# Windowed self-attention of a decoder in plain fp32 on heads padded to 32 rows, two units a step

## The reference

```python
qkv = hidden_states @ w_qkv.T
q, k, v = jnp.split(qkv, 3, axis=-1)
q = _rms_norm(q, q_norm_w); k = _rms_norm(k, k_norm_w)     # over all 256 columns
# 16 heads of 16 columns
q = _rope(q); k = _rope(k)
mask = (q_idx >= k_idx) & (q_idx - k_idx <= 127)
scores = jnp.where(mask, einsum('bhqd,bhkd->bhqk', q, k) / 4, -inf)
probs = softmax(scores)
out = einsum('bhqk,bhkd->bhqd', probs, v) @ w_o.T
```

## Time and profile before

| what | us |
|---|---|
| median of 3 runs | 1463.75 |
| the three runs | 1457.23, 1463.75, 1466.10 |
| the profiled execution, its own time | 1464.83 |
| its span, first to last instruction | 1463.0 |
| mean granted TensorE clock, share of full | 0.922 |
| instructions | 22043 |

### The profile page before, as it was taken

How to read it: one execution, slowest core, us unless ns; L and a number is a source line. 1 busy time by engine, 2 the same in 40 slices (tenths; PEclk the granted TensorE clock), 3 DMA queues, 4 the chain that set the end, 5 groups by cost and what they waited for, 6 DMA issues and landing times.

```text
span 1463.0 us, 22043 instructions
## 1 busy us (share of the span) xinstructions
PE 1228.0 (84%) x7024; PEld 833.0 (57%) x7024; DVE 924.3 (63%) x2269; ACT 590.8 (40%) x1524; POOL 547.2 (37%) x629
## 2 busy tenths in 40 slices
PE   7688998999869877689989999999999806988881
PEld 3554664677634365557768336643566705777770
DVE  1678886653697975839964877668765442544443
ACT  2247775884531102548820137621665122222220
POOL 2243773642242314525520004410343172444444
PEclk9899999999769978989997999999999957999996
DMA  7165994000001001010020000000400442544444
GB/s 284 56 225 169 327 316 135 2 1 1 30 1 43 1 1 72 0 58 2 2 107 17 0 0 1 2 0 1 201 2 35 181 175 69 84 85 81 82 75 104
DMA packets 69615, 110.75 MB, mean 76 GB/s; under 512 B 5056, under 2 KB 59840, under 8 KB 66240
## 3 DMA queue, kind: packets, MB, share of 16 engines
q1 hardware_dynamic: 58896, 96.62, 19.5%
q0 software_dynamic: 10608, 12.72, 5.7%
HBM read 57.41 MB, written 51.91 MB: 75 GB/s over the span
## 4 chain that ended last, share of the span: by engine, by line
PE 62%; DVE 18%; issue 6%; POOL 6%; DMA 4%; ACT 3%; SPq 0%; POOLq 0%; DVEq 0%; ACTq 0%
PE ps L692 8%; PE ps L681 6%; PE ps L967 6%; PE ps L701 4%; PE ps L673 4%; PE ps L674 3%; PE ps L1021 3%; PE ps L1018 3%; DMA sums<-mem 2%; PE ps L948 2%; PE ps L641 2%; PE ps L803 2%; POOL mem L1858 2%; DVE mem L1155 1%; PE ps L786 1%
## 5 line engine op out<-in xcount | busy, mean ns | idle before, releaser
L1858 POOL TENSOR_SCALAR mem<-mem 128x512 f32<-128x512 f32 x256 | 177.6, 698 | 388.6 <-DVE mem L1160 385.3
L1155 DVE TENSOR_REDUCE mem<-ps 128x1 f32<-128x512 f32 x256 | 175.2, 686 | 108.9 <-PE ps L674 100.4
L1670 ACT ACTIVATE mem<-ps,mem 128x512 f32<-128x512 f32 x256 | 177.1, 696 | 12.7 <-DVE mem L1155 12.1
L681 PE MATMUL ps<-mem 128*128 128x128 f32 x1024 | 159.0, 278 | 14.3 <-POOL mem L1858 13.4
L681 PEld LDWEIGHTS ps<-mem 128*128 128x128 f32 x1024 | 118.1, 141 | 69.5 <-POOL mem L1858 50.7
L1663 ACT ACTIVATE mem<-ps 128x512 f32<-128x512 f32 x192 | 116.0, 606 | 93.2 <-PE ps L681 92.7
L1924 POOL DMA_INDIRECT sums<-mem x63 | 97.1, 1541 | 128.3 <-DVE mem L1532 102.3
L673 PE MATMUL ps<-rounded_at 128*128 128x512 f32 x256 | 124.3, 486 | 11.8 <-DVE rounded_at L1144 10.4
L692 PE MATMUL ps<-mem 128*64 128x256 f32 x1024 | 125.8, 388 | 2.4 <-ACT mem L1663 2.4
L1868 POOL TENSOR_TENSOR mem<-mem 128x512 f32<-128x512 f32 x40 | 55.4, 1384 | 140.5 <-DVE mem L1196 140.4
L1638 ACT ACTIVATE rounded_at<-ps 64x512 fp32r<-64x512 f32 x64 | 37.8, 591 | 167.1 <-PE ps L950 154.3
(11 more groups left out here) (259 smaller groups left out, 2646.7 us busy)
## 6 DMA issues: line engine op xcount, KB each, us to landing
slots<-mem SPq DMA_DIRECT2D x15, 2312.0 KB, 9.9
mem<-in_f_w_dram SPq DMA_DIRECT2D x16, 1024.0 KB, 10.3
mem<-slots SPq DMA_DIRECT2D x63, 136.0 KB, 2.5
mem<-in_f_w_dram SPq DMA_DIRECT2D x24, 256.0 KB, 3.3
mem<-in_x_wq_dram SPq DMA_DIRECT2D x2, 2048.0 KB, 13.2
mem<-in_x_wo_dram SPq DMA_DIRECT2D x2, 2048.0 KB, 8.3
mem<-sums SPq DMA_DIRECT2D x8, 256.0 KB, 4.6
mem<-in_x_wqr_dram SPq DMA_DIRECT2D x1, 1536.0 KB, 6.7
```

Of the source, the lines that this page charges most:

```text
L681: mm = pe.transpose(ps[3 + j % 2][:, k * P:(k + 1) * P], PR[j % 6][:, k * P:(k + 1) * P], ident)
L1155: dve.tensor_reduce(nmax[:, i % 8:i % 8 + 1], ps[SB[lay][i % len(SB[lay])]][:, :], AX.X, ALU.max, negate=True)\
L1670: act.activation(PR[i % 6], ps[SB[lay][i % len(SB[lay])]][:, :], ACT.Exp, bias=nmax[:, i % 8:i % 8 + 1], accum_out=esum[:, i % 8:i % 8 + 1 ...
L1858: pool.tensor_scalar(PR[i % 6], PR[i % 6], rinv[:, i % 8:i % 8 + 1], 1.0, ALU.mult, ALU.mult)\
```

## The change

Only the fourth sublayer changes. There are no high and low parts any more: Q, K, V and the probabilities stay plain fp32, and their products have two passes. A head's 16 columns are padded with zeros to 32 (`QK1`), so four heads stand under each other after one transpose of 128 columns, at rows 0, 32, 64 and 96; a tile takes 8 transposes instead of 16, and one copy each by ACT and DVE instead of three and one. The banks of the transposed tiles are doubled. The cosine product moves from POOL to DVE; POOL clears the padding once and the padding of V at the end.

The loop goes over 24 pairs. The two units of a pair (hh = 0, 1) take heads at neighbouring row groups and write neighbouring banks of one double bank `pp`. DVE takes one maximum over both (1024 columns) and one reciprocal; ACT has all exponentials of a pair; POOL still makes one product a unit. The transposed probabilities are copied once, by DVE in kind 0 and for hh = 1, by ACT else. Products with V write rows 32 (h // 4), and the output copy of a unit has 128 or 64 rows and 128 columns; the two copies stand at the head of DVE's step, for pair m-4. `keep_clock` is gone: the mask product of a pair's first unit is repeated KEEP_FIRST = 6 times in the first three pairs and KEEP = 1 time later. The rows of `a1_wo` are reordered on the host to suit.

```diff
@@ program
-        ps = [ctx.enter_context(nc.psum_tensor(f"ps{i}", [P, 512], F32)) for i in range(8)]
+        pp = [ctx.enter_context(nc.psum_tensor(f"ps{i}", [P, 1024], F32)) for i in range(4)]
+        ps = [pp[i // 2][:, i % 2 * 512:(i % 2 + 1) * 512] for i in range(8)]
+        QK1 = [at(144 + 4 * i, 2 * NH1 * 32, pattern="p (h d) -> p h d", d=32) for i in range(2)]
+                e = "dve" if hh == 1 or window_pair(m)[1] == 0 else "act"
@@ PE
                 def transposes(t):
+                    pe.wait_ge(a1_qp, t + 1)
+                    if t >= 2:
+                        pe.wait_ge(a1_tev, t - 1)
+                        pe.wait_ge(a1_tev_d, t - 1)
+                    for a2 in range(2):
+                        for c in range(4):
+                            mm = pe.transpose(ps[4 + 2 * (t % 2) + a2][:, c * P:(c + 1) * P],
+                                              QK1[t % 2][:, 16 * a2 + 4 * c:16 * a2 + 4 * c + 4, :].rearrange("p h d -> p (h d)"), ident)
...
+                for m in range(PAIRS1 + 3):
+                    if m < PAIRS1:
...
+                        if m >= 2:
+                            pe.wait_ge(a1_ex, 2 * m - 2)
+                        for hh in [0] * (KEEP_FIRST if m < 3 else KEEP) + [0, 1]:
+                            pe.matmul(ps[2 * (m % 2) + hh], identb, mask.unsqueeze(1).to_broadcast([P, g, 512 // g]), start=True, stop=False,
+                                      skip_group_check=True)
+                        for c in range(g):
+                            for hh in range(2):
+                                dst, rows = ps[2 * (m % 2) + hh], slice(32 * (i + hh), 32 * (i + hh) + 32)
...
+                    j = m - 2
+                    if 0 <= j < PAIRS1:
+                        for hh in range(2):
+                            pe.wait_ge(a1_nm, 2 * j + hh + 1)
+                            if j >= 1:
+                                copied(j - 1, hh)
...
+                    v = m - 3
...
+                                    mm = pe.matmul(ps[6 + hh][r:r + 32, 0:P], V1[2 * b + kt][:, h, :, :].rearrange("p v d -> p (v d)"),
+                                                   PT1[(2 * v + hh) % 4][:, cc * P:(cc + 1) * P], start=kt == 0, stop=kind == 0 or kt == 1)
@@ DVE, preparation
-                        dve.wait_ge(a1_vh, t + 1)
-                        low_values(t)
...
-                        dve.wait_ge(a1_ra, t + 1)
+                        step(dve.tensor_tensor(ra.rearrange("p (h d) -> p h d", d=HD1), src,
+                                               rope1[:, 0, t % 2:t % 2 + 1, :].to_broadcast([P, 32, HD1]), ALU.mult))
...
-                        low_q(t - 1)
@@ DVE, pairs
+                for m in range(PAIRS1 + 4):
+                    v = m - 4
+                    if 0 <= v:
...
+                        for hh in range(2):
+                            dve.wait_ge(a1_pv, 2 * v + hh + 1)
+                            dve.tensor_copy(aT1[rows, i + hh, s0:s0 + P], ps[6 + hh][rows, 0:P]).then_inc(a1_ao, 1)
+                    if m < PAIRS1:
+                        b, kind, i, g = window_pair(m)
+                        dve.wait_ge(a1_s, m + 1)
+                        dve.tensor_reduce(mx1[m % 4][:, 0:2 * g], pp[m % 2][:, :].rearrange("p (g w) -> p g w", g=2 * g),
                                           AX.X, ALU.max, negate=True).then_inc(a1_mx, 1)
@@ POOL, preparation
+                for i in range(2):
+                    last = pool.memset(QK1[i][:, :, HD1:32], 0.0)
+                last.then_inc(a1_pad, 1)
...
+                pool.memset(V1pad, 0.0).then_inc(a1_vpad, 1)
```

More of the change, by code:

```diff
@@ L271, in program, with window_pair @@
         mhalf2 = col(2)
-        mx1, es1, rc1 = ([col(4) for _ in range(4)] for _ in range(3))
+        mx1, es1, rc1 = ([at(142 + 0.25 * k + 0.0625 * i, 16) for i in range(4)] for k in range(3))
         U1 = 12 * B
+        PAIRS1 = U1 // 2
+        KEEP_FIRST, KEEP = 6, 1
+        def window_pair(m):
+            b, kind, i = m // 6, m // 2 % 3, 2 * (m % 2)
+            return b, kind, i, 4 if kind == 0 else 2
+        window_copy, copies1 = {}, {"act": 0, "dve": 0}
+        for m in range(PAIRS1):
+            for hh in range(2):
+                e = "dve" if hh == 1 or window_pair(m)[1] == 0 else "act"
+                copies1[e] += 1
+                window_copy[m, hh] = e, copies1[e]
         wq_1 = at(136, H * D, pattern="p (h d) -> p h d", h=H)
@@ L837, in window_attention, with copied @@
                 transposes(NT - 1)
+                def copied(m, hh):
+                    e, n = window_copy[m, hh]
+                    pe.wait_ge(a1_cd if e == "dve" else a1_ca, n)
                 pe.wait_ge(a1_mb, 1)
[L840 to L842 removed]
+                for m in range(PAIRS1 + 3):
+                    if m < PAIRS1:
+                        b, kind, i, g = window_pair(m)
+                        if m == 0:
@@ L867, in window_attention @@
[L867 to L890, removed]
@@ new lines, in window_attention @@
+                        act.activation(qS[j // 2][:, :, (j % 2) * P:(j % 2 + 1) * P],
+                                       ps[4 + 2 * (j % 2)].rearrange("p (c s) -> p c s", c=4), ACT.Copy).then_inc(a1_tev, 1)
+                for m in range(PAIRS1 + 2):
+                    j = m - 2
+                    if 0 <= j < PAIRS1:
+                        for hh in range(2):
+                            if window_copy[j, hh][0] == "act":
+                                act.wait_ge(a1_t, 2 * j + hh + 1)
+                                if j >= 2:
+                                    act.wait_ge(a1_pv, 2 * j - 3 + hh)
+                                act.activation(PT1[(2 * j + hh) % 4], ps[4 + hh], ACT.Copy).then_inc(a1_ca, 1)
+                    if m < PAIRS1:
+                        b, kind, i, g = window_pair(m)
+                        act.wait_ge(a1_mx, m + 1)
+                        if m >= 3:
+                            act.wait_ge(a1_t, 2 * m - 4)
+                        w = 512 // g
+                        for hh in range(2):
+                            for c in range(g):
+                                last = act.activation(pr1[(2 * m + hh) % 6][:, c * w:(c + 1) * w], ps[2 * (m % 2) + hh][:, c * w:(c + 1) * w], ACT.Exp,
+                                                      bias=mx1[m % 4][:, g * hh + c:g * hh + c + 1],
+                                                      accum_out=es1[m % 4][:, g * hh + c:g * hh + c + 1])
+                            last.then_inc(a1_ex, 1)
@@ new lines, in window_attention @@
+                for t in range(NT):
+                    pool.wait_ge(a1_sq, t + 1)
+                    pool.tensor_scalar(sse1[:, t, 0:1], ss1[:, t, 0:1], HD1 / D, RMS_EPS * HD1, ALU.mult, ALU.add)
+                    step(pool.tensor_scalar(sse1[:, t, 1:2], ss1[:, t, 1:2], 1.0 / D, RMS_EPS, ALU.mult, ALU.add))
+                    pool.tensor_tensor(rs1[:, t, :], sse1[:, t, :], mhalf2, ALU.pow).then_inc(a1_rs, 1)
+                pool.memset(V1pad, 0.0).then_inc(a1_vpad, 1)
+                for m in range(PAIRS1):
+                    g = window_pair(m)[3]
+                    pool.wait_ge(a1_rc, m + 1)
+                    for hh in range(2):
+                        v = pr1[(2 * m + hh) % 6].rearrange("p (g w) -> p g w", g=g)
+                        pool.tensor_tensor(v, v, rc1[m % 4][:, g * hh:g * hh + g].unsqueeze(2).to_broadcast([P, g, 512 // g]), ALU.mult)\
+                            .then_inc(a1_nm, 1)
```

210 lines of the change are left out of this document (62 added, 148 removed).

## The result

The changed kernel takes 1423.0 us (median of 4 runs, 1417.9 to 1424.4) against 1460.8 for the kernel before beside it: 0.974 of it, 95% interval 0.969 to 0.978. That is 37.8 us less; forecast were 33.8 less and 1430. The profiled execution took 1424.44 us.

What follows compares the result with a forecast made beforehand. Prediction: a relay over engines bounds the preparation and DVE the units; PE would bound the pairs. From the profiled 1464.8, 32 us (preparation) and 2.5 (pairs) come off: 1430.3, median called 1430, range 1420 to 1452.

Steps and rivals of the forecast that it cites:

- Preparation: Stretch before the pairs: DVE bound at 3.8 us a tile, PE 3.5; 38.5 us instead of 70.4.
- rival E: Preparation: DVE and POOL still hold each other up, 24 us more, kernel 1454; chance 0.04.
- C: Rival, preparation: PE stays at half clock, 7.0 us a tile, kernel 1452; chance 0.06.
- The waits are loose: Preparation: transposes of tile t need only the copies of t-2, and its products the scaling of t-2; no separate size.
- Pairs: Loop over 24 pairs: PE bound, 3.82 us a pair in kinds 1 and 2, 4.72 in kind 0; 104.5 us.
- B: Rival, pairs: row groups run one at a time, scores of kinds 1 and 2 1.73 us, kernel 1440; chance 0.17.
- D: Rival, pairs: loads not hidden, scores 2.6 us (kinds 1, 2) and 3.5 (kind 0), kernel 1466 or 1495; chance 0.09.
- Scores of kind 0: Pairs, PE: 16 passes of 128 columns at 0.112 us, set by weight loads, plus 0.2; 2.0 us a pair.
- Products with V of kind 0: Pairs, PE: 16 passes at 0.059 us, four column groups in turn, plus 0.05; 0.99 us a pair.
- The start: First three pairs: five more mask products each, at 0.216 us; 3.2 us together.
- The output copies at the head: Head of DVE's step, pair m-4: 0.54 us while PE does masks and scores for 1.85; costs nothing.
- The repeated mask product: Pairs: lies on PE's path, 21 products at 0.216 us; 4.5 of the 104.5 us.

Runs made afterwards that it cites:

- e7: Changed kernel with transposes of tile t waiting for the copies of tile t-1 again, banks still doubled: preparation 47.8 us, whole 1425.9 us (one run).
- b1: Kernel before with only the cosine product moved from POOL to DVE: preparation 65.0 us, whole 1458.1 us, ratio 0.999.
- e5: Changed kernel with the cosine product back on POOL: preparation 44.1 us, whole 1427.7 us.
- e6: Changed kernel with each output copy of the pairs made twice by DVE: pairs 98.7 us, whole 1419.2 us.
- e3: Changed kernel with a pair's score products ordered unit by unit instead of alternating: pairs 103.0 us, whole 1426.2 us.
- e4: Changed kernel with the two output copies at the end of DVE's step instead of its head: pairs 145.5 us, whole 1482.7 us, 1.018 of the kernel before.
- e1: Changed kernel without the repeated mask product from the fourth pair on: pairs 94.1 us, whole 1414.2 us.
- c1: Changed kernel with ten unread identity products before each of the preparation's last two transpose groups: pairs 95.4 us, whole 1416.7 us.

## Why the prediction was right, and where not

**Preparation: right, 38.5 forecast, 38.5 measured.** DVE's tile came at 3.64 us for 3.8. It bounds the second half of the stretch, PE the first; the forecast had put them 0.3 apart. No DVE product is stretched, which ends rival E; the half clock came only in the first 3.5 us, as priced, and at the end, which ends C. That the sum is exact is luck: the start to the first scaling took 6.7 us for 6.5, the eight tiles 28.8 for 30.4, the last transposes with their wait 2.1 for 0.9, since they ran at half clock, and the last copy with its wait 0.9 for 0.7. One sign that was named did not come: DVE was to be busy over 80% of the stretch and was busy 74% (28.51 of 38.50 us), because it idles until its first scaling; from there on it is 90%. The account of the gain was not whole either. "The waits are loose" holds for the kernel as changed, but the doubled banks that make them so carry 9.3 us (e7), and the cosine product, to which the forecast gave the most words, 5.6 (b1; e5 has the same size).

**Pairs: mechanism right, 104.5 forecast, 98.5 measured**, outside the 101 to 108 that were named as the sign, with steps of 3.41 to 3.87 us for 3.8 and 4.7. PE took the bound over from DVE (chain after, e6), rows in turn run side by side, the loads do not show: rivals B and D fall with 1.06 us for the scores of kinds 1 and 2 against a forecast of 1.1 (1.73 and 2.6 for the rivals). Masks 0.75 and transposes 1.02 fit their terms (0.75, 0.98). Three terms were mis-sized:
- Scores of kind 0: 1.09 us, not 2.0; 8 pairs, 7.3 us less, the largest miss., 0.112 us a pass of 64 columns on two row groups in turn, were read as one weight load at full clock, 16 of them one behind the other. The same place of the table by stretches, kernel before, says otherwise:

```profile
59.70:63.30 3.60, 3.54 (x32) 3.42 (x32) 3.39 (x8) 0.00 (x0) 1.50 (x2) 0.53 0.00 0
```

 The granted clock there is 0.53. At half clock 0.112 us are about 0.056 at full, and 16 x 0.056 + 0.2 is the 1.1 that was measured. Whether those 0.056 are stream or load, alone can't tell. The kernel before has the case that tells, on a single row group and at clock 1.00:

```profile
765.40 0.66 PE L918 MATMUL ps<-mem 64*128 64x64 f32 x4
```

 Its passes of 64 columns start 0.112 us apart (765.561, 765.673, 765.784), twice their stream of 0.054. So there is a price of about 0.112 us a pass in one row group, most likely the load's, and it has two ways to vanish that the forecast left out: two row groups in turn pay it side by side, and a stream of 128 columns (0.108) covers it. If load and stream were paid in turn, 128 columns would cost 0.054 more than 64 here; e3 shows 0.112 for them too, on a group of 32 rows. The prediction said that no row of its trace has passes behind each other on one row group; L918 has them.
- Products with V of kind 0: 0.57 us, not 0.99; 8 pairs, 3.4 less. Four column groups in turn cost 0.036 a pass, two (kinds 1 and 2) 0.0625, as assumed for all.
- The start: it was priced at full clock. 16 masks took 3.57 + 3.52 us for 3.46, two rounds of scores 2.01 + 1.22 for 2.18: 4.7 us more.

 -7.3 - 3.4 + 4.7 = -6.0, and the stretch was 6.0 shorter than forecast. That it closes to the tenth is again in part luck: transposes at 1.02 instead of 0.98 add 1.0 us, and the 2.3 for the end of the pairs, not tested by themselves, were about 1 too much (PE stood idle for 1.2 us of the whole stretch).

**The output copies at the head: "nothing", and right**, with the condition that the prediction named ("if PE gave pair m-4 later, each step would lose it"). e4 shows its other side: at the end of the step each step loses 1.3 us or more, 47 in all with the clock.

**The repeated mask product: 4.5 us forecast, 4.4 measured** (e1). That it could simply go was not asked.

## What to carry to other kernels

Read the granted clock beside every price taken from a trace; a duration from a stretch at 0.53 is not a price at full clock. A price for parts of the array that work in turn holds for that alternation: ask what one of them costs alone. When a chain runs round over several engines, look for the item that closes the ring (here the last copy of a tile, and the output copy) and give it a second bank or an earlier place: this moved 9 and 47 us without changing the work. An engine that waits in front of a dense stretch pays again inside it at half clock; unread products cost nothing while it waits anyway, but one that stands on the path of a busy PE costs its full time.

## What the runs showed of the hardware

- PE starts fp32 passes of another 32-row group ahead of up to three earlier ones of its list: order is free at 4 passes a unit, costs 0.55 us at 8 (e3, all 24 pairs).
- Two 32-row groups side by side: 8 passes of 256 columns in 1.06 us, 16 of 128 in 1.09. A single group: 0.112 us a pass of 128 columns, load included (e3), and no less for 64 columns on a 64-row group (L918, kernel before).
- Column groups in turn: 16 passes of 128 columns in 1.00 us with two, 0.57 with four.
- The same DVE product takes 424 ns alone and up to 1495 beside a POOL product of its kind, and POOL's cosine product 1.51 us; in the kernel after, where POOL makes only its small factors beside them, none took over 427.
- Two waits of PE of 2.57 us each, at the end of the preparation, stood before 14 us at 1.2 GHz. With products in these waits the stretch stayed at 2.4 GHz (c1).
